# Row-by-row fetches in a graph kernel's last three aggregations: every 12th pair instead of every 14th

## What is computed

```
h = relu(layernorm(x))
x = x + L2(h):   agg[type, dst] += edge_weight * h[src]     # 8 relations
                 out = sum over relations of agg[r] @ blockdiag(W[r])
h = relu(layernorm(x))
x = x + L3(h):   twice:  h = relu(h @ w1 + b1)
                         agg[dst] += edge_weight * h[src]
                         h = relu(batchnorm(agg @ w2 + b2)) # and a second batch norm
```

## Time and profile before

| what | value |
| --- | --- |
| median of 3 runs | 3314.28 us (3305.43 to 3316.3) |
| span of the profiled execution | 3318.0 us, 3.7 us above the median |
| GpSimd (POOL) busy | 2386.1 us, 72% |
| TensorE (PE) busy | 2189.3 us, 66% |
| VectorE (DVE) busy | 2090.3 us, 63% |
| ScalarE (ACT) busy | 1413.4 us, 43% |
| first to last gather, first of the three aggregations | 1765.8 to 2240.1 us |
| second | 2259.2 to 2733.5 us |
| third | 2789.8 to 3264.0 us |

### The profile page before, as it was taken

The page is one execution under the profiler, slowest core; times in us unless marked ns, Lnnn a source line. Parts: engine busy times, 40 slices in busy tenths (PEclk is TensorE's granted clock), DMA queues, the critical chain, the costliest instruction groups (busy, mean ns, idle before and its releaser), DMA issues. The chain is left out here.

```text
span 3318.0 us, 73877 instructions
## 1 busy us (share of the span) xinstructions
PE 2189.3 (66%) x11487; PEld 1592.8 (48%) x11488; DVE 2090.3 (63%) x5467; ACT 1413.4 (43%) x4736; POOL 2386.1 (72%) x2419
## 2 busy tenths in 40 slices
PE   6566377776656367766696666676666677666667
PEld 2455255555455355555443444454444456444446
DVE  8899867766489967776694444464444454444446
ACT  2666399998566479988581000031000014000004
POOL 7877777777777767777655777775777773777773
PEclk9799699998889789999797778687777798777788
DMA  5488734443688745443694333443333332333332
GB/s 165 132 228 226 215 111 141 140 127 105 174 227 227 214 118 163 142 130 104 161 283 159 109 109 109 125 125 108 109 109 109 108 104 78 110 109 110 109 107 79
DMA packets 346744, 466.05 MB, mean 140 GB/s; under 512 B 111879, under 2 KB 262248, under 8 KB 343184
## 3 DMA queue, kind: packets, MB, share of 16 engines
q0 software_dynamic: 111952, 284.59, 29.8%
q1 hardware_dynamic: 161584, 111.23, 11.5%
q10 hardware_dynamic: 72852, 67.08, 7.5%
HBM read 385.50 MB, written 76.97 MB: 139 GB/s over the span
## 5 line engine op out<-in xcount | busy, mean ns | idle before, releaser
L400 PE MATMUL t_ps<-t_ring,shared 128*128 x2640 | 900.5, 494 | 499.2 <-ACTq L237 418.3
L400 PEld LDWEIGHTS t_ps<-t_ring,shared 128*128 128x128 f32 x2640 | 601.8, 244 | 787.5 <-issue 697.4
L186 POOL DMA_INDIRECT ring<-feat_d,srcC x784 | 772.3, 985 | 264.8 <-issue 215.2
L186 POOL DMA_INDIRECT t_ring<-feat_d,srcC x758 | 719.7, 950 | 289.3 <-issue 215.5
L265 ACT ACTIVATE ring<-ring,exC 128x64 f32<-128x64 f32 x3136 | 788.0, 335 | 0.2
L400 PE MATMUL bank<-ring,arena 128*128 x1408 | 426.9, 428 | 166.7 <-ACT ring L265 117.8
L318 DVE TENSOR_TENSOR acc<-acc,t_ps 128x256 f32 x440 | 185.3, 421 | 504.3 <-PE t_ps L400 502.9
L608 POOL DMA_INDIRECT attr_d<-abuf,attr_pos x392 | 401.9, 1025 | 117.7 <-issue 117.7
L186 POOL DMA_INDIRECT t_ring<-rel_d,relC x379 | 360.0, 950 | 160.6 <-issue 107.4
L302 DVE TENSOR_SCALAR shared<-lane,dlocT,weightT 128x128 f32<-128x128 f32 x1320 | 406.4, 360 | 50.9 <-issue 31.9
L1828 ACT COPY t_ring<-t_pt 128x512 f32<-128x512 f32 (+1 forms) x14 | 7.8, 554 | 883.3 <-PE t_pt L1795 883.3
(11 more groups left out here) (297 smaller groups left out, 2715.3 us busy)
## 6 DMA issues: line engine op xcount, KB each, us to landing
arena<-lo_d ACTq DMA_DIRECT2D x392, 128.0 KB
rel_d<-mid_stage SPq DMA_DIRECT2D x25, 1024.0 KB, 4.7
arena<-attr_d SPq DMA_DIRECT2D x98, 260.0 KB, 2.9
abuf<-in_attr SPq DMA_DIRECT2D x56, 448.0 KB
t_ring<-feat_d SPq DMA_DIRECT2D x1536, 1.0 KB
t_ring<-feat_d ACTq DMA_DIRECT2D x1536, 1.0 KB
ring<-feat_d,srcC POOLq DMA_INDIRECT x784
t_ring<-rel_d SPq DMA_DIRECT2D x768, 1.0 KB
```

The costliest lines, as they stand in the source:

```text
L186: pool.indirect_dma_start(out=ring[:, u % RING, j, 0:D], out_offset=None, in_=table, in_offset=bass.IndirectOffsetOnAxis(ap=index[:, u, j: ...
L400: last = pe.matmul(ps[k % len(ps)][:, 0:g.width], hot[:, k % NHOT, j, :], ring[:, slot, j, 0:g.width], start=(j == 0), stop=(j == 1))
```

## The change

Four numbers. Pairs by row come every 12th instead of every 14th pair, so `BY_ROW` holds 14 pairs (12, 24, ..., 168) instead of 12 (14, 28, ..., 168). SyncE fetches 68 of the 128 rows instead of 64, ScalarE 60 instead of 64. SyncE's 68 rows are loaded into registers as 32, 32 and 4, where they were 32 and 32; ScalarE's 60 as 32 and 28, from byte 272 of the row of indices instead of byte 256. The last-step numbers are loaded 16 registers at a time, each time from a multiple of 64 bytes, instead of 14 from multiples of 56 bytes. ScalarE's share is 5 rows in each pair, where it was 4 or 5. The sizes of `row_src`, `row_type`, `row_rel` and of the index transfer (L1906 to L1908) follow.

```diff
@@ -38,16 +38,16 @@
 BIG = 1.0e30
 LN_EPS = 1e-5
 BN_EPS = 1e-5
-ROW_STEP = 14
+ROW_STEP = 12
 NOTES = 172
 PEEL = 2
 SAFE = PAIRS
 ACT_TILES = 10
 BY_ROW = tuple(range(ROW_STEP, NOTES, ROW_STEP))
-SP_ROWS = 64
+SP_ROWS = 68
 ROW_REGS = 32
 ROW = 4 * D
-LASTS = 14
+LASTS = 16
```

## The result

The changed kernel takes 3350.83 us (median of 4 runs, 3349.97 to 3351.3) against 3311.03 us of the kernel before, run beside it (4 runs, 3305.43 to 3316.3). The ratio is 1.0123, with a 95% interval of 1.0108 to 1.0137: 1.2% slower, where I had forecast 3309.8 and a range up to 3323. The profiled execution has a span of 3348.2 us.

The account below looks back on a forecast made before the run. GpSimd's gathers were taken to bound each aggregation: 2.5 us saved in each of three, less 3.0 lost to ScalarE's lateness in the first, -4.5 us; 3313.5 profiled, 3309.8 as median, range 3301 to 3323.

Parts of the forecast that it names:

- the tight part of the sum: ScalarE's queue of rows, loads and notes: it falls behind GpSimd by 0.35 us per 12 pairs, or 0.8.
- (b): ScalarE bounds all three aggregations: each round 0.6 us dearer, about 3323.6 us; chance 0.18, of which 0.02 the far end.
- Sum per 48 pairs: ScalarE's rows, notes, loads and landing waits: 116.9 us (118.7 in the first aggregation) against GpSimd's 115.5.
- The place of the payment: GpSimd's wait for ScalarE's notes at pair 172, where it meets ScalarE's lateness once per aggregation.
- The point up to which ScalarE may be late: ScalarE's note 172 may come until 421.3 us after GpSimd's start in the changed kernel.
- SyncE under cover: SyncE's batch of 68 rows with a third load costs 27.2 us, within GpSimd's 28.9 for 12 pairs.
- ScalarE late at pair 12 by its own landing: ScalarE begins 2.5 to 3 us late at pair 12, waiting for rows it has just issued.
- in the second and third aggregation nothing is lost: There ScalarE's note 172 comes at 416.7 us, before the 421.3 limit, so GpSimd does not stop.
- The forecast's net for the three aggregations: GpSimd gains 2.5 us in each aggregation and loses 3.0 in the first: -4.5 us in all.
- (a): ScalarE's added work is all hidden, landings taking 2.3 us everywhere: the full -7.5 us, 3306.8 us; chance 0.30.
- (c): TensorE's own late work ends each aggregation, so GpSimd's earlier finish buys nothing: 3314 us; chance 0.10.
- (d): SyncE bounds through its third load, 29.0 us a batch, 0.1 over GpSimd's round, costing only together with (b); chance 0.02.

Follow-up runs that it names:

- e9: Changed kernel with ScalarE's rows issued two pairs ahead and SyncE fetching 64 rows instead of 68: 3307.58 us, 0.9990 of the kernel before.
- e6: Changed kernel with the rows split 64 to 64 between SyncE and ScalarE, as before the change: 3393.37 us, 1.0240 of the kernel before.
- e10: Changed kernel with SyncE fetching 40 rows singly and 28 (wrong ones) by one DMA, ScalarE's queue untouched: 3302.07 us, 0.9975 of the kernel before.
- e1: Changed kernel with SyncE fetching 72 rows instead of 68, ScalarE 56: 3306.6 us, 0.9978 of the kernel before.
- e5: Changed kernel with ScalarE's rows issued two pairs ahead, same rows, loads and notes: 3304.15 us, 0.9979 of the kernel before.
- e2: Changed kernel with ScalarE's 60 rows spread over the first 10 of the 12 pairs: 3335.64 us, 1.0074 of the kernel before.
- e8: Kernel before with only the loads of last steps changed, 16 registers at a time instead of 14: 3308.56 us, 0.9990 of the kernel before.
- e7: Changed kernel with last steps loaded 14 registers at a time, as before the change: 3390.0 us, 1.0240 of the kernel before.

## Why the prediction was wrong

The mechanism was in it, both as the tight part of the sum and as rival (b), and the experiments bear it out point by point. What failed is the size of one sum, "Sum per 48 pairs: ... = 116.9 us in the second and third aggregation, 118.7 in the first": 122.2 and 124.4 us measured, 4.5% and 4.8% more. The rows, the notes, the index loads and the loads of last steps were all put too low.

**What was right.** Two gathers less in each aggregation, 1.254 us each, and GpSimd's pace the same. The place of the payment, the wait at L199 before note 172. The point up to which ScalarE may be late: 421.3 us by the earlier trace rows, about 421.7 by e9. SyncE under cover in spite of its third load: its batch took 27.5 us (27.2 predicted). No price for index loads from byte 272: 2.14 us there, and the same from byte 256 in e6. ScalarE late at pair 12 by its own landing. TensorE and VectorE only moved along.

**What was wrong.** The terms of ScalarE's 13 rounds in the second aggregation, predicted and measured:

| term | predicted us | measured us |
| --- | --- | --- |
| 780 rows | 249.6 (0.320 each) | 254.8 (0.327) |
| 156 notes | 34.3 (0.220 each) | 36.7 (0.235) |
| 26 index loads | 51.0 (1.96) | 53.6 (2.06) |
| slow first issues and gaps behind loads | 7.0 (26) | 9.2 (33) |
| loads of last steps | 8.3 (7 of 1.18) | 13.0 (10 of 1.30) |
| waits for its own rows | 29.9 | 29.9 |
| sum | 380.1 | 397.2 |

Each row is 7 ns dearer than the 0.320 that I had taken, and each note 15 ns dearer. SyncE's batch in the earlier trace rows had given 0.323, which I rounded down, and the notes came from one stretch of 10 us. The kernel before has 0.326 a row over the whole of its second aggregation, so this number was there to be read. The index loads of 32 registers took 2.14 us: 1.97 is what they take behind a load of last steps, as nearly all first loads did before. Those of 28 took 2.02, while my own source for them, 1.74, would have given 17.1 for the eight and not the 17.9 that I wrote. The issue behind a load of last steps is slow too, which I had counted for index loads alone. The three loads of last steps that coincide with a pair by row were counted as free: the wait behind them is 0.87 to 1.9 us, so they shorten it less than they last. That the waits come out at 29.9 in both columns is luck: I had 13 of 2.3 us, and there were ten of 2.56 on average and three, behind these loads, of 0.85 to 1.9. None of the errors is large, all have one sign, and all are multiplied by 13. In the first aggregation the waits add to it, 37.4 us against 35.8.

The lateness is a difference of two near equals. I predicted 0.35 us a round, 29.2 less 28.85, and got 1.7: an error of 4.5% of a round makes what adds up nearly five times as large. Pair 168 was noted 2699.6 + 0.8 - 2268.8 = 431.6 us after the first gather and landed near the 408.4 of the forecast: 23 us late, not 7.6. And behind the threshold each further microsecond is paid in full, three times. So "in the second and third aggregation nothing is lost" became 12.6 and 15 us. The forecast's net for the three aggregations, +0.5, -2.5 and -2.5, was +18.1, +9.7 and +11.9.

**The rivals.** (b) is what happened, with a price of 40 us where I had 9.3 (3323.6): I had let a round be 0.6 us dearer, it was 1.3. (a) failed by the same sum as the forecast. It asks for landings of 2.3 us, a wait of 2.1 at each pair by row; the second aggregation had 2.3 on average, and 13 x 0.2 = 2.6 us less would still have put note 172 at 430.5, 9 us too late. Waits of 1.1 to 1.6 us, as in e10, come with next to no loss. The 2.0 us of the Trainium skill (DMA: Bandwidth & Descriptors, Anatomy of one DMA) lies between those waits and the 2.3 of the changed kernel, and by it the prediction had the full gain, which is not what came. (c) is wrong: GpSimd's finish moved the end of the kernel nearly one to one, up in the changed kernel, down in e1 and e5; from the last gather to the end it is 53.1 to 53.2 us in all three and 54.0 before. (d) is wrong: SyncE had issued its last row for pair 168 31 us before ScalarE issued its own, and e5 loses nothing with the same batches and the same third load.

**The chances.** The check of the sum on the kernel before could not have caught the error. It gave 62.1 us against 67.8, and the 5.7 us in which ScalarE waits for gathers would have hidden a sum that is up to 9% low. The range should have been made from this. Already 4% of 30 us is 1.2 us a round and 16 us at note 172, hence stops of 11, 11 and 18 us, which less the gain reaches about 3347.

## What to carry over

When two queues run in step and one comes within a few per cent of the other, the forecast is of their difference times the number of rounds, and it needs the sum of a round to be known more closely than that difference. Where it can't be had so well, forecast the threshold, and count the far side in full. A check of the sum on a kernel in which that queue has slack proves little: fit it to a stretch in which the queue never waits.

A wait for one's own last transfer was hidden here by issuing the next batch's first transfers meanwhile (e5), not by stopping earlier (e2): the late queue passed two empty slots in 0.45 us. And an aid that is worth nothing where the engine has slack (16 registers a load, e8) was worth 40 us where it had none (e7).

## What the hardware showed beside

**Register loads.** Loads of 4 registers took 0.56 us and of 8 0.79 on SyncE's queue; on ScalarE's, loads of 16 from a multiple of 64 bytes took 1.30, of 24 1.68, of 28 2.02 here and 1.74 elsewhere; loads of 32 took 1.97 to 2.16 on both (medians by place). On VectorE 4 took 0.35. So 4 registers are dearer on SyncE than on VectorE, and near the floor of about 600 ns that the Trainium skill (DMA: Bandwidth & Descriptors, Latency and other measured facts) gives; the two engines differ, and I had taken the wrong one. Loads of 14 took 3.3 to 3.5 us when they started at an odd multiple of 56 bytes, which is no multiple of 16, and 1.5 to 1.6 at the even ones (112, 224, ...); the first, at byte 0, took 1.2 (the earlier trace rows has one of each).

**A queue's own landing depends on what the other queue does.** The changed kernel has both kinds itself. At the 30 pairs by row where no load stood ahead and SyncE's last row had gone out at most 2 us before ScalarE's last one, ScalarE waited 1.9 to 4.1 us for its own rows; at pair 168, for which SyncE's last row had gone out 31 us before, 0.8 to 0.9. In e10, with SyncE silent for 9 us or more, 29 such waits took 0.9 to 1.6 us and one 3.2 (pair 156 of the first aggregation, unexplained). It is not the issuing of SyncE as such: in e6, at pair 60 of the second aggregation, SyncE had issued its last row 2.6 us before ScalarE's last, and the wait was still long (the last two issues of SyncE's batch, which end at 2446.43, and the wait that begins at 2449.2).

```profile
2445.88 0.55 SPq L206 DMA_DIRECT2D t_ring<-feat_d  x2
...
L237 ACTq EVENT_SEMAPHORE  x1: 2537/2537/2537, 2449.2 to 2449.2; - x1
```

In the second and third aggregation of e6 the waits of pairs 60, 108 and 156 (SyncE's last row 2.4 to 2.7 us before) took 2.5 to 2.9 us, those of pairs 72, 84, 120 and 132 (4.4 to 4.8 us before) 0.9 to 1.5. That points at SyncE's rows still under way; how they delay the other queue's completion is open.
